# A transformer layer on eight cores: the bias moved from TensorE to VectorE, the residual load moved to GpSimd's queue, three staging buffers in place of four

## The chip, the cores and the metric

The kernel runs on all 8 cores of one Trainium2 chip, each core with one batch element and the whole set of weights. No core talks to another, but they share the chip's memory. The metric is the device time of the slowest core, in microseconds (us). The core profiled in detail is core 1.

## The reference

Per batch element, with x of 2048 rows (S) by 2048 columns (E) in f32:

```python
xn = _layernorm(x, axis=-1)
# attention: 16 heads of 128, rope on q and k, causal softmax
q = (x @ wq).reshape(B, S, H, D)      # here x is xn
...
attn = jax.nn.softmax(scores, axis=-1)
out = jnp.einsum('bhqk,bkhd->bqhd', attn, v).reshape(B, S, E)
return out @ wo
# ffn: ternary weights
scale = jnp.mean(jnp.abs(weight))
w_t = jnp.clip(jnp.round(weight / (scale + EPS)), -1.0, 1.0)
...
return jnp.einsum('bsi,oi->bso', x, w_ste) + bias
# the layer
x = x + attn_part + ffn_part
```

So the result is a sum of four things: the residual x, attention's output times wo, xn times the quantized ffn weight, and the bias, one value per column.

## The kernel before, in words

The kernel is written engine by engine: a Python planner appends closures to five lists (SyncE, ScalarE, VectorE, TensorE, GpSimd), and every instruction of an engine runs in the order in which it was appended. Semaphores carry all dependencies, each counted by the planner. The helper `dma` (line 150 issues a plain transfer, line 148 a transposing one) puts on the named engine's list the waits, then the transfer. A transfer that waits therefore holds up all that stands behind it on that engine.

**Start.** SyncE loads eight constants (rope tables c2 and s2 of 1 MB each, then six small ones) on one semaphore `c`, each after the one before has landed. GpSimd's queue holds the bias row `biasb`, then the first four tiles of x into `xst[0..3]` (128 rows, 1 MB each), then the weights of heads 0 and 1 (`wslq`, `wslk`, `wslv`, 0.5 MB each as bf16, cast on the way).

**Layernorm** (`plan_ln_tile`, 16 tiles). GpSimd loads x into `xst[b]`, b the tile's number mod 4, once the tile that used it last is done. ScalarE makes sum and sum of squares (L191, L198), VectorE mean and variance (L208 to L222), ScalarE the inverse root (L229, L236), VectorE the normalized bf16 tile `xnn` (L243), and SyncE transposes it by DMA into `xnT`, which stays in SBUF. VectorE's list begins with a wait for all constants, ahead of its first L208. Four tiles are planned ahead of head 0, and four more behind each of its chunks.

**Heads.** Each of 16 heads has four chunks of 512 rows: projections k, q, v from `xnT` and the head's weights (L474, L477) into the banks pA and pB, rope on VectorE, v transposed by DMA, then scores, Exp and the products with v. Between the chunks stand parts of the weight quantization: `plan_quantA_tile` (heads 2 to 5, ScalarE sums |w|) and `plan_quantB_tile` (heads 6 to 13, VectorE). Both load `wf` into the same `xst` buffers by GpSimd's queue. The quantized, transposed weight goes to DRAM as `wtT_scr`; the heads' outputs go to `outT_scr`, the last two heads' stay in `oTs`.

**Phase 2.** SyncE loads `oTh[0]` (rows 0 to 1023 of the heads' output), ScalarE's queue `oTh[1]`, 14 transfers each. The output is made in 16 chunks: two halves of the rows by eight column blocks of 256 (W2). Chunk idx needs `woc` (a block of wo, cast to bf16 on GpSimd's queue) and `wtc` (a block of the quantized weight, on SyncE's), two buffers each. `plan_ph2_weights(idx + 1)` stands in the lists ahead of the tiles of chunk idx, and its transfers wait until TensorE is done with chunk idx - 1, whose buffers they take. A chunk has eight tiles of 128 rows. For each tile SyncE loads `xsl`, the residual's 128x256 block (two buffers, each free when VectorE is done with its last tile), and TensorE makes 33 matmuls into one of two PSUM banks:

- L922, one matmul with one row: ones times the bias row, which starts the sum;
- L930, 16 matmuls of the heads' output and `woc`;
- L933 and L937, 16 matmuls of `xnT` and `wtc`.

VectorE adds `xsl` to the bank and writes `osl` (L953), ScalarE's queue stores `osl` to y. TensorE may write a bank again when VectorE has read it, so it runs two tiles ahead of VectorE and no more.

Of the kernel before, what the change touches and what calls it, by code (L numbers as in the profile page):

```python
# [8 lines left out]
F32 = mybir.dt.float32  # L9
# [5 lines left out]
E = 2048  # L15
# [24 lines left out]
def build_nc():  # L40
# [26 lines left out]
    with ctx:  # L67
# [8 lines left out]
        onrf = sb("onrfs", [1, 128], F32)  # L76
        biasb = sb("biasb", [1, E], BF16)
        st6 = sb("st6", [128, 24], F32)
        mv = [sb(f"mv{i}", [128, 2], F32) for i in range(4)]
        rstd = [sb(f"rstd{i}", [128, 1], F32) for i in range(4)]  # L80
        epsv = sb("epsv", [128, 1], F32)
        bias3 = sb("bias3", [128, 1], F32)
        accw = sb("accw", [128, 16], F32)
# [2 lines left out]
        thrv = sb("thrv", [128, 1], F32)  # L86
        nthrv = sb("nthrv", [128, 1], F32)
        oTs = [sb(f"oTs{i}", [128, S], BF16) for i in range(2)]
        ctx1 = ExitStack()
        sb1 = lambda n_, s_, d_: ctx1.enter_context(nc.sbuf_tensor(n_, s_, d_))  # L90
        xst = [sb1(f"xst{i}", [128, E], F32) for i in range(4)]
        xnn = [sb1(f"xnn{i}", [128, E], BF16) for i in range(2)]
        wtbf = [sb1("wtbf0", [128, E], BF16)] * 4
        wtTs = [sb1("wtTs0", [128, NT * 128], BF16)] * 4
# [66 lines left out]
        def _(e):  # L161
            e.memset(epsv[:, :], LN_EPS)
            e.memset(bias3[:, :], -3.0)
            e.wait_ge(sems["c"], consts_c)

        @on("tensor")
        def _(e):
            e.wait_ge(sems["c"], consts_c)

        xst_free = [("dv", 0), ("dv", 0), ("dv", 0), ("dv", 0)]  # L170
        xnn_free = [("txn", 0), ("txb", 0)]
        ln_state = {"prev_aggr": 0}
        ln_prev = [0, 0, 0, 0]

        def plan_ln_tile(tt):
            b = tt % 4
            b2 = tt % 2
            xs = "x%d" % b
            my_x = dma("gpsimd", xs,
                       (lambda tt=tt, b=b: (xst[b][:, :],  # L180
                        bass.AP(x_d.tensor, tt * 128 * E, [[E, 128], [1, E]]), False)),
                       extra_waits=[xst_free[b]])

            @on("scalar")
            def _(e, b=b, b2=b2, xs=xs, my_x=my_x, xf=xnn_free[b2], prev=ln_prev[b]):
                e.wait_ge(sems[xs], my_x)
                if xf:
                    e.wait_ge(sems[xf[0]], xf[1])
                if prev:
                    e.wait_ge(sems["dv"], prev)  # L190
                e.activation(out=xnn[b2][:, :], in_=xst[b][:, :], func=AF.Copy,  # L191
                             accum_out=mv[b][:, 0:1]).then_inc(sems["ac"], 1)
            ac_copy = bump("ac")

            @on("scalar")
            def _(e, b=b, b2=b2, ac_copy=ac_copy):
                e.wait_ge(sems["ac"], ac_copy)
                e.activation(out=xnn[b2][:, :], in_=xst[b][:, :], func=AF.Square,  # L198
                             accum_out=mv[b][:, 1:2]).then_inc(sems["ac"], 1)
            ac_sums = bump("ac")  # L200

            dv_m = bump("dv")
            dv_var1 = bump("dv")

            @on("vector")
            def _(e, b=b, ac_sums=ac_sums, dv_m=dv_m):
                e.wait_ge(sems["ac"], ac_sums)
                e.tensor_scalar(out=mv[b][:, 0:1], in0=mv[b][:, 0:1], scalar1=1.0 / E,  # L208
                                scalar2=None, op0=ALU.mult).then_inc(sems["dv"], 1)
                e.wait_ge(sems["dv"], dv_m)  # L210
                e.scalar_tensor_tensor(out=st6[:, b:b + 1], in0=mv[b][:, 0:1], scalar=-1.0,
                                       in1=mv[b][:, 0:1], op0=ALU.mult,
                                       op1=ALU.mult).then_inc(sems["dv"], 1)
            bump_chk = cnt["dv"]
            assert bump_chk == dv_var1

            dv_var2 = bump("dv")

            @on("vector")
            def _(e, b=b, dv_var1=dv_var1):  # L220
                e.wait_ge(sems["dv"], dv_var1)
                e.tensor_scalar(out=rstd[b][:, :], in0=mv[b][:, 1:2], scalar1=1.0 / E,  # L222
                                scalar2=st6[:, b:b + 1], op0=ALU.mult,
                                op1=ALU.add).then_inc(sems["dv"], 1)

            @on("scalar")
            def _(e, b=b, dv_var2=dv_var2):
                e.wait_ge(sems["dv"], dv_var2)
                e.activation(out=rstd[b][:, :], in_=rstd[b][:, :], func=AF.Ln,  # L229
                             bias=epsv[:, :]).then_inc(sems["ac"], 1)  # L230
            ac_ln = bump("ac")

            @on("scalar")
            def _(e, b=b, ac_ln=ac_ln):
                e.wait_ge(sems["ac"], ac_ln)
                e.activation(out=rstd[b][:, :], in_=rstd[b][:, :], func=AF.Exp,  # L236
                             scale=-0.5).then_inc(sems["ac"], 1)
            ac_rstd = bump("ac")

            @on("vector")  # L240
            def _(e, b=b, b2=b2, ac_rstd=ac_rstd):
                e.wait_ge(sems["ac"], ac_rstd)
                e.tensor_scalar(out=xnn[b2][:, :], in0=xst[b][:, :], scalar1=mv[b][:, 0:1],  # L243
                                scalar2=rstd[b][:, :], op0=ALU.subtract,
                                op1=ALU.mult).then_inc(sems["dv"], 1)
            dv_xn = bump("dv")
            xst_free[b] = ("dv", dv_xn)
            ln_prev[b] = dv_xn

            txs = "txn" if tt % 2 == 0 else "txb"  # L250
            xnn_free[b2] = (txs, dma("sync", txs,
                              (lambda tt=tt, b2=b2: (
                                  bass.AP(xnT, tt * 128, [[NT * S, 128], [S, NT], [1, 128]]),
                                  xnn[b2][:, :], True)),
                              extra_waits=[("dv", dv_xn)]))
# [8 lines left out]
        quantB_state = {"prev_sub": 0}  # L264

        def plan_quantA_tile(qt):
            b = qt % 4
            b2 = qt % 2
            xs = "x%d" % b
            my_x = dma("gpsimd", xs,  # L270
                       (lambda qt=qt, b=b: (xst[b][:, :],
                        bass.AP(wf_d.tensor, qt * 128 * E, [[E, 128], [1, E]]), False)),
                       extra_waits=[xst_free[b]])

            @on("scalar")
            def _(e, qt=qt, b=b, b2=b2, xs=xs, my_x=my_x):
                e.wait_ge(sems[xs], my_x)
                e.wait_ge(sems["txn"], xnT_ready)
                e.wait_ge(sems["txb"], xnT_ready)
                e.activation(out=xnn[b2][:, :], in_=xst[b][:, :], func=AF.Abs,  # L280
                             accum_out=accw[:, qt:qt + 1]).then_inc(sems["ac"], 1)
            qa_ac[qt] = bump("ac")
            xst_free[b] = ("ac", qa_ac[qt])
# [56 lines left out]
            return bump("dv")  # L340

        def plan_quantB_tile(qt, thr_dv):
            b = qt % 4
            xs = "x%d" % b
            my_x = dma("gpsimd", xs,
                       (lambda qt=qt, b=b: (xst[b][:, :],
# [537 lines left out]
        for idx in range(len(chunks)):  # L884
# [7 lines left out]
            if True:  # L892

                for ti in range(8):
# [3 lines left out]
                    syp = "sy%d" % tb  # L898
                    pp = ph2_psums[tb]
                    xsl_first = (half == 0 and ec == 0 and ti < 2)  # L900
                    xsl_ld = dma("sync", xsp,
                                 (lambda tt=tt, tb=tb, ec=ec: (xsl[tb][:, :],
                                  bass.AP(x_d.tensor, tt * 128 * E + ec * W2, [[E, 128], [1, W2]]),
                                  False)),
# [4 lines left out]
                    def _(e, pp=pp, ti=ti, tt=tt, ec=ec, ecb=ecb, wop=wop, wcp=wcp,  # L909
# [9 lines left out]
                        e.wait_ge(sems["bias"], bias_v)  # L919
                        if dv_gate:  # L920
                            e.wait_ge(sems["dv"], dv_gate)
                        e.matmul(pp[:, 0:W2], onr[:, :], biasb[0:1, ec * W2:(ec + 1) * W2],  # L922
                                 start=True, stop=False)
                        for it in range(NT):
                            if it >= H - 2:
                                lh = oTs[it % 2][:, tt * 128:(tt + 1) * 128]
                            else:
                                lh = bass.AP(oTh[half], it * 1024 + ti * 128,
                                             [[H * 1024, 128], [1, 128]])
                            e.matmul(pp[:, 0:W2], lh,  # L930
                                     woc[ecb][:, it * W2:(it + 1) * W2], start=False, stop=False)
                        for it in range(NT - 1):
                            e.matmul(pp[:, 0:W2],  # L933
                                     bass.AP(xnT, it * S + tt * 128, [[NT * S, 128], [1, 128]]),
# [8 lines left out]
                    wtc_used_pe[ecb] = pe_out  # L943


                    @on("vector")
                    def _(e, pp=pp, tb=tb, xsp=xsp, syp=syp, pe_out=pe_out,
                          xsl_ld=xsl_ld, osl_gate=osl_st[tb]):
                        e.wait_ge(sems["pe"], pe_out)
                        e.wait_ge(sems[xsp], xsl_ld)  # L950
                        if osl_gate:
                            e.wait_ge(sems[syp], osl_gate)
                        e.tensor_tensor(out=osl[tb][:, :], in0=pp[:, 0:W2], in1=xsl[tb][:, :],  # L953
                                        op=ALU.add).then_inc(sems["dv"], 1)
                    dv_out = bump("dv")
                    ph2_free_dv[tb] = dv_out
# [87 lines left out]
```

## Time and profile before

| | us |
|---|---|
| Three timed runs | 2002.83, 1991.86, 1933.22 (median 1991.86) |
| Profiled execution, its own time | 1938.87 |
| Its span on the slowest core (core 1) | 1937.1 |
| Spans of the eight cores | 1869.6 to 1937.1 |
| TensorE busy, core 1 | 1574.5 (81% of the span) |
| VectorE busy | 671.5 |
| ScalarE busy | 538.0 |

On core 1 the program falls into three parts: layernorm and its transposes with heads 0 and 1 (0 to about 300 us), the other heads (to 1353 us), and phase 2 (1353 to 1937 us). A busy share is an average over all three, so each part is read by itself. In rows, PE is TensorE, PEld its weight loads, DVE VectorE, ACT ScalarE, POOL GpSimd, and SPq, ACTq the DMA-issuing queues of SyncE and ScalarE. All DMAs issued by the helper carry its line, 150 or 148, and are told apart by their tiles.

### The profile page before, as it was taken

How to read it: one execution, taken by the hardware profiler on the slowest of the kernel's cores; microseconds unless marked ns; L12 is line 12 of the kernel's file. 1: busy time of each engine (PE TensorE's matmuls, PEld its weight loads, DVE VectorE, ACT ScalarE, POOL GpSimd, SP SyncE). 2: the span in 40 equal slices, each digit the busy share in tenths (PEclk: the TensorE clock that was granted, in tenths of full speed). 3: DMA queues.
4: the chain of work that ended last, by engine and by line, in shares of the span. 5: the costliest groups of instructions: out<-in, count | busy, mean ns of one | idle time of the engine just before them, and what ended most of it. 6: DMA issues, size and time to landing. Idle time of an engine off the chain costs nothing. (4 is left out here: it accounts for less than half of the span.)

```text
span 1937.1 us, 29502 instructions; the slowest of 8 cores (1869.6 to 1937.1 us)
## 1 busy us (share of the span) xinstructions
PE 1574.5 (81%) x9220; PEld 885.1 (46%) x9220; DVE 671.5 (35%) x1399; ACT 538.0 (28%) x897; POOL 100.4 (5%) x117
## 2 busy tenths in 40 slices
PE   0044359999999999999999999998369999999999
PEld 0011123444444444444444444443257787777777
DVE  0123243346445556546546645543000110101101
ACT  1311345463554353343344235144000000000000
POOL 2000001000101000000000000000000000000000
PEclk9986689999999999999999999999689999999999
DMA  9967729027536364465356245000954655555462
GB/s 191 117 83 73 134 47 161 28 82 131 91 92 98 87 123 72 98 115 79 93 115 107 63 71 85 20 9 8 232 109 104 140 124 130 126 132 126 109 153 66
DMA packets 350388, 194.93 MB, mean 101 GB/s; under 512 B 240163, under 2 KB 338468, under 8 KB 343844
## 3 DMA queue, kind: packets, MB, share of 16 engines
q0 software_dynamic: 139040, 92.29, 28.9%
q1 hardware_dynamic: 190756, 80.31, 20.2%
q10 hardware_dynamic: 20448, 20.46, 3.2%
q8 instruction: 85, 1.39, 0.3%
q14 instruction: 59, 0.48, 0.1%
HBM read 177.28 MB, written 32.51 MB: 108 GB/s over the span
## 5 line engine op out<-in xcount | busy, mean ns | idle before, releaser
L577 ACT ACTIVATE et<-pC,bias 128x512 bf16<-128x512 f32 (+3 forms) x240 | 149.9, 625 | 595.1 <-PE pC L564 594.0
L614 PE MATMUL pF<-et,onms 128*128 128x512 bf16 (+3 forms) x640 | 223.3, 351 | 16.1 <-ACT et L577 12.2
L474 PE MATMUL pA<-xnT,wslk 128*128 128x512 bf16 x480 | 115.6, 396 | 126.7 <-DMA xnT<-xnn 126.5
L474 PE MATMUL pB<-xnT,wslv 128*128 128x512 bf16 x480 | 115.0, 394 | 79.1 <-DVE prawk L489 79.1
L953 DVE TENSOR_TENSOR osl<-pA,xsl 128x256 f32<-128x256 f32 x64 | 27.2, 425 | 366.5 <-PE pA L937 183.1
L588 DVE TENSOR_TENSOR et<-et,trim 128x128 bf16<-128x128 bf16 x256 | 57.3, 225 | 269.7 <-ACT et L577 265.9
L616 PE MATMUL pG<-et,vh 128*128 128x512 bf16 (+3 forms) x384 | 135.8, 357 | 0.0
L577 ACT ACTIVATE et<-pD,bias 128x512 bf16<-128x512 f32 (+3 forms) x208 | 130.8, 629 | 2.0 <-PE pD L564 0.9
L474 PEld LDWEIGHTS pA<-xnT,wslk 128*128 128x128 bf16 x480 | 46.7, 101 | 183.8 <-issue 137.1
L564 PE MATMUL pC<-qTh,kTh 128*128 128x512 bf16 (+3 forms) x240 | 83.9, 349 | 55.9 <-ACT et L577 55.9
L577 ACT ACTIVATE et<-pH,bias 128x512 bf16<-128x512 f32 (+1 forms) x192 | 118.6, 618 | 2.0 <-PE pH L564 1.8
L930 PE MATMUL pA<-woc,oTh 128*128 128x256 bf16 x896 | 118.9, 289 | 0.0
L933 PE MATMUL pA<-wtc,xnT 128*128 128x256 bf16 x960 | 118.9, 278 | 0.0
L933 PE MATMUL pB<-wtc,xnT 128*128 128x256 bf16 x960 | 115.3, 273 | 0.0
L614 PEld LDWEIGHTS pF<-et,onms 128*128 128x128 bf16 x640 | 62.6, 98 | 114.2 <-issue 67.2
L474 PEld LDWEIGHTS pB<-xnT,wslv 128*128 128x128 bf16 x480 | 48.2, 101 | 141.2 <-issue 88.8
L930 PE MATMUL pB<-woc,oTh 128*128 128x256 bf16 x896 | 108.9, 273 | 0.0
L474 PE MATMUL pA<-xnT,wslq 128*128 128x512 bf16 x480 | 108.8, 379 | 0.0
L474 PE MATMUL pA<-xnT,wslv 128*128 128x512 bf16 x480 | 108.8, 379 | 0.0
L474 PE MATMUL pB<-xnT,wslq 128*128 128x512 bf16 x480 | 108.8, 379 | 0.0
L474 PE MATMUL pB<-xnT,wslk 128*128 128x512 bf16 x480 | 108.8, 379 | 0.0
L933 PEld LDWEIGHTS pA<-wtc,xnT 128*128 128x128 bf16 x960 | 96.1, 100 | 13.4
(97 smaller groups left out, 1956.6 us busy)
## 6 DMA issues: line engine op xcount, KB each, us to landing
xst<-wf POOLq DMA_DIRECT2D x32, 1024.0 KB, 12.1
xst<-x POOLq DMA_DIRECT2D x16, 1024.0 KB, 15.2
woc<-wo POOLq DMA_DIRECT2D x16, 1024.0 KB, 13.3
wtc<-wtT_scr SPq DMA_DIRECT2D x16, 1024.0 KB, 7.1
xsl<-x SPq DMA_DIRECT2D x128, 128.0 KB, 3.1
y<-osl ACTq DMA_DIRECT2D x128, 128.0 KB, 2.9
wslq<-wq POOLq DMA_DIRECT2D x16, 512.0 KB, 8.0
wslk<-wk POOLq DMA_DIRECT2D x16, 512.0 KB, 9.7
```

The costliest lines, as they stand in the source:

```text
L474: e.matmul(pp[:, 0:CW], wsl[:, it * 128:(it + 1) * 128], bass.AP(xnT, it * S + c * CW, [[NT * S, 128], [1, CW]]), start=(it == 0), stop=False)
L564: e.matmul(pc_[:, col0:CW], kTh[hb][:, kt * 128:(kt + 1) * 128], bass.AP(qTh[hb], cs0 + col0, [[S, 128], [1, n]]), start=True, stop=True). ...
L577: e.activation(out=et[slot][:, col0:CW], in_=pc_[:, col0:CW], func=AF.Exp, scale=INV_SQRT_D, bias=bias3[:, :]).then_inc(sems["ac"], 1)
L588: e.tensor_tensor(out=et[slot][:, col0:col0 + 128], in0=et[slot][:, col0:col0 + 128], in1=tri[:, :], op=ALU.mult).then_inc(sems["dv"], 1)
L614: e.matmul(pF[:, col0:CW], onm[:, :], et[slot][:, col0:CW], start=(kt == 0), stop=(kt == nkt - 1))
L616: e.matmul(pv[:, col0:CW], vh[hb][:, kt * 128:(kt + 1) * 128], et[slot][:, col0:CW], start=(kt == 0), stop=(kt == nkt - 1)).then_inc(sems[ ...
L930: e.matmul(pp[:, 0:W2], lh, woc[ecb][:, it * W2:(it + 1) * W2], start=False, stop=False)
L933: e.matmul(pp[:, 0:W2], bass.AP(xnT, it * S + tt * 128, [[NT * S, 128], [1, 128]]), wtc[ecb][:, it * W2:(it + 1) * W2], start=False, stop= ...
L953: e.tensor_tensor(out=osl[tb][:, :], in0=pp[:, 0:W2], in1=xsl[tb][:, :], op=ALU.add).then_inc(sems["dv"], 1)
```

## The change

Four edits, and what they bring with them.

1. `xst`, `mv` and `rstd` have three buffers in place of four, and all `% 4` of the tiles become `% 3`.
2. A tile `biasbc` (128 x 2048, bf16) holds the bias on all partitions. It is filled at the start: four matmuls of ones and a quarter of `biasb` into pH, each copied out by ScalarE, one after the other. They stand ahead of layernorm on both engines.
3. In phase 2 the bias matmul is gone, and VectorE adds `biasbc` in a second instruction behind the first. TensorE and the next `xsl` load wait for the second one.
4. The `xsl` loads are issued by GpSimd in place of SyncE.

```diff
-        xst = [sb1(f"xst{i}", [128, E], F32) for i in range(4)]
+        xst = [sb1(f"xst{i}", [128, E], F32) for i in range(3)]
...
+        biasbc = sb("biasbc", [128, E], BF16)
...
+        for j in range(4):
+            @on("tensor")
+            def _(e, j=j, bv=bias_v, pba=prev_bb_ac):
+                if j == 0:
+                    e.wait_ge(sems["c"], consts_c)
+                    e.wait_ge(sems["bias"], bv)
+                else:
+                    e.wait_ge(sems["ac"], pba)
+                e.matmul(pH[:, 0:512], onr[:, :], biasb[0:1, j * 512:(j + 1) * 512],
+                         start=True, stop=True).then_inc(sems["pe"], 1)
+            pe_bb = bump("pe")
+
+            @on("scalar")
+            def _(e, j=j, pe_bb=pe_bb):
+                e.wait_ge(sems["pe"], pe_bb)
+                e.activation(out=biasbc[:, j * 512:(j + 1) * 512], in_=pH[:, 0:512],
+                             func=AF.Copy).then_inc(sems["ac"], 1)
+            prev_bb_ac = bump("ac")
...
-            b = tt % 4
+            b = tt % 3
...
-                    xsl_ld = dma("sync", xsp,
+                    xsl_ld = dma("gpsimd", xsp,
...
-                        e.matmul(pp[:, 0:W2], onr[:, :], biasb[0:1, ec * W2:(ec + 1) * W2],
-                                 start=True, stop=False)
...
-                                     woc[ecb][:, it * W2:(it + 1) * W2], start=False, stop=False)
+                                     woc[ecb][:, it * W2:(it + 1) * W2], start=(it == 0), stop=False)
...
                         e.tensor_tensor(out=osl[tb][:, :], in0=pp[:, 0:W2], in1=xsl[tb][:, :],
+                                        op=ALU.add).then_inc(sems["dv"], 1)
+                        e.wait_ge(sems["dv"], dv_out1)
+                        e.tensor_tensor(out=osl[tb][:, :], in0=osl[tb][:, :],
+                                        in1=biasbc[:, ec * W2:(ec + 1) * W2],
                                         op=ALU.add).then_inc(sems["dv"], 1)
```

**GpSimd's queue in phase 2.** Before, from the first loads of phase 2 on (line 150 is the helper's; `waits` names the semaphores, `wo0` and `wo1` those of woc's own buffers, pe TensorE's):

```order
L150 DMA woc0<-wo 128x16x256 [waits so0,so1,sw0,sw1,tv0,tv1,tw0,tw1,txn,txb,pe,dv]
L150 DMA woc1<-wo 128x16x256 [waits so0,so1,sw0,sw1,tv0,tv1,tw0,tw1,txn,txb,pe,dv]
L150 DMA woc0<-wo 128x16x256 [waits pe,wo0]
```

In the changed kernel, around the load of chunk 2's block, which stands ahead of the eight tiles of chunk 1 (the helper's line is 151 now, xs0 and xs1 are the semaphores of the two `xsl` buffers, dv is VectorE's):

```order
L151 DMA xsl1<-x 128x256 [waits dv,xs1]
L151 DMA woc0<-wo 128x16x256 [waits pe,wo0]
L151 DMA xsl0<-x 128x256 [waits dv,xs0]
L151 DMA xsl1<-x 128x256 [waits dv,xs1]
L151 DMA xsl0<-x 128x256 [waits dv,xs0]
L151 DMA xsl1<-x 128x256 [waits dv,xs1]
L151 DMA xsl0<-x 128x256 [waits dv,xs0]
L151 DMA xsl1<-x 128x256 [waits dv,xs1]
L151 DMA xsl0<-x 128x256 [waits dv,xs0]
L151 DMA xsl1<-x 128x256 [waits dv,xs1]
L151 DMA woc1<-wo 128x16x256 [waits pe,wo1]
L151 DMA xsl0<-x 128x256 [waits dv,xs0]
```

The eight residual loads of each chunk have come to stand between two `woc` loads. On SyncE's queue they stood in the same way behind `wtc`; before, at the same place of the program:

```order
L150 DMA xsl1<-x 128x256 [waits dv,xs1]
L150 DMA wtc0<-wtT_scr 128x16x256 [waits sw0,sw1,pe,wc0]
L150 DMA xsl0<-x 128x256 [waits dv,xs0]
L150 DMA xsl1<-x 128x256 [waits dv,xs1]
L150 DMA xsl0<-x 128x256 [waits dv,xs0]
```

So a residual load leaves the queue behind one block load, and joins the queue behind the other.

**GpSimd's queue at the start.** Before, from the bias row on (x0 to x3 are the semaphores of the `xst` buffers, a load that waits for dv waits until VectorE has normalized the tile in that buffer):

```order
L150 DMA xst2<-x 128x2048
L150 DMA xst3<-x 128x2048
L150 DMA wslq0<-wq 128x16x128
L150 DMA wslk0<-wk 128x16x128
L150 DMA wslv0<-wv 128x16x128
L150 DMA wslq1<-wq 128x16x128 [waits wq]
```

And now:

```order
L151 DMA xst2<-x 128x2048
L151 DMA xst0<-x 128x2048 [waits dv,x0]
L151 DMA wslq0<-wq 128x16x128
L151 DMA wslk0<-wk 128x16x128
L151 DMA wslv0<-wv 128x16x128
L151 DMA wslq1<-wq 128x16x128 [waits wq]
```

The fourth tile's load has become one that waits for tile 0's layernorm, and all weights of heads 0 and 1 stand behind it.

## Rows read from the trace of the kernel before

**Rows 1.** Stretches: PE, PEld, DVE, ACT, POOL busy us (instructions), granted clock, DMA share, GB/s.

```profile
0.00:20.00 20.00, 0.00 (x0) 0.00 (x0) 0.09 (x2) 5.29 (x5) 6.44 (x12) 1.00 0.88 262
17.00:50.00 33.00, 0.00 (x0) 0.00 (x0) 0.00 (x0) 0.47 (x2) 3.43 (x3) 1.00 1.25 157
55.00:111.00 56.00, 0.00 (x0) 0.01 (x1) 6.39 (x13) 16.76 (x22) 2.15 (x4) 1.00 1.06 113
300.00:1353.00 1053.00, 978.39 (x4620) 437.72 (x4618) 538.50 (x1104) 455.18 (x782) 65.32 (x74) 0.99 0.45 84
1420.00:1937.00 517.00, 482.28 (x4078) 392.91 (x4076) 52.67 (x124) 0.00 (x0) 15.98 (x14) 0.98 0.54 120
```

**Rows 2.** Chain of waits, 1420 to 1937 us, its shares by line.

```profile
by line: DMA xsl<-x 23.0%; PE pA L930 18.1%; PE pB L930 16.8%; PE pA L933 15.4%; PE pB L933 14.9%; PE pA L922 2.1%; PE pB L922 1.9%; DMA y<-osl 1.4%; DVE osl L953 1.3%; issue 1.3%; PE pB L937 1.0%; SPq L150 1.0%; PE pA L937 1.0%; SPq L143 0
```

**Rows 3.** The same chain at one chunk boundary: start us, us, what.

```profile
1536.02 0.21 PE pB L922
1536.23 1.85 PE pB L930 x16
1538.08 1.64 PE pB L933 x15
1539.72 0.12 PE pB L937
...
1540.49 7.71 DMA xsl<-x
...
1548.36 0.43 DVE osl L953
...
1548.93 0.26 PE pA L922
```

**Rows 4.** Waits by total, 1420 to 1937 us: us, times, longest.

```profile
PE pA L922 <- DVE osl L953: 31.9, 15, 4.7
```

**Rows 5.** The page's DMA issues: transfers, KB each, median us from issue to landing.

```profile
woc<-wo POOLq DMA_DIRECT2D x16, 1024.0 KB, 13.3
wtc<-wtT_scr SPq DMA_DIRECT2D x16, 1024.0 KB, 7.1
xsl<-x SPq DMA_DIRECT2D x128, 128.0 KB, 3.1
```

**Rows 6.** DMA issues at two other boundaries, near 1471 and 1705 us: slowest and fastest.

```profile
woc<-wo POOLq DMA_DIRECT2D x1, 1024.0 KB, 15.9
...
woc<-wo POOLq DMA_DIRECT2D x1, 1024.0 KB, 12.1
```

**Rows 7.** GpSimd's DMA issues from 299.5 us, 1.16 us apart: first and third.

```profile
wslq<-wq POOLq DMA_DIRECT2D x1, 512.0 KB, 8.3
...
wslv<-wv POOLq DMA_DIRECT2D x1, 512.0 KB, 11.8
```

**Rows 8.** Chain of waits in phase 2: first tile behind the longest stop, then behind a shorter.

```profile
1416.96 3.52 PE pA L930 x16
1420.48 2.62 PE pA L933 x15
...
1446.68 3.33 PE pA L930 x16
```

**Rows 9.** TensorE behind the longest stop: stretch as in rows 1, and its first instruction.

```profile
1416.60:1420.40 3.80, 3.80 (x18) 2.52 (x19) 0.18 (x1) 0.00 (x0) 0.00 (x0) 0.50 0.50 145
...
1416.59 0.36 PE L922 MATMUL pA<-biasb,onrs 1*128 1x256 bf16 x1 [12.65 <-DVE osl L953]
```

**Rows 10.** The start in order of time: start us, us, engine, instruction.

```profile
20.13 0.33 SPq L150 DMA_DIRECT2D trim<-tri  x1
45.77 0.30 SPq L150 DMA_DIRECT2D onrs<-onr  x1
52.88 0.15 DVE L208 TENSOR_SCALAR mv<-mv 128x1 f32<-128x1 f32 x1 [51.65 <-DMA onms<-onm]
111.02 5.38 PE L474 MATMUL pA<-xnT,wslk 128*128 128x512 bf16 x15 [111.02 <-DMA xnT<-xnn]
```

More of the change, by code:

```diff
@@ L78, in build_nc @@
         st6 = sb("st6", [128, 24], F32)
-        mv = [sb(f"mv{i}", [128, 2], F32) for i in range(4)]
-        rstd = [sb(f"rstd{i}", [128, 1], F32) for i in range(4)]
+        mv = [sb(f"mv{i}", [128, 2], F32) for i in range(3)]
+        rstd = [sb(f"rstd{i}", [128, 1], F32) for i in range(3)]
         epsv = sb("epsv", [128, 1], F32)
@@ L164, in _ @@
             e.wait_ge(sems["c"], consts_c)
+        prev_bb_ac = 0
+        for j in range(4):
[15 more added lines that the diff above has]
+            prev_bb_ac = bump("ac")
+        biasbc_ac = cnt["ac"]
         @on("tensor")
@@ L168, in _ @@
             e.wait_ge(sems["c"], consts_c)
-        xst_free = [("dv", 0), ("dv", 0), ("dv", 0), ("dv", 0)]
+        xst_free = [("dv", 0), ("dv", 0), ("dv", 0)]
         xnn_free = [("txn", 0), ("txb", 0)]
         ln_state = {"prev_aggr": 0}
-        ln_prev = [0, 0, 0, 0]
+        ln_prev = [0, 0, 0]
         def plan_ln_tile(tt):
-            b = tt % 4
+            b = tt % 3
             b2 = tt % 2
@@ L266, in plan_quantA_tile @@
         def plan_quantA_tile(qt):
-            b = qt % 4
+            b = qt % 3
             b2 = qt % 2
@@ L342, in plan_quantB_tile @@
         def plan_quantB_tile(qt, thr_dv):
-            b = qt % 4
+            b = qt % 3
             xs = "x%d" % b
@@ L943, in build_nc, with _ @@
                     wtc_used_pe[ecb] = pe_out
+                    dv_out1 = bump("dv")
                     @on("vector")
-                    def _(e, pp=pp, tb=tb, xsp=xsp, syp=syp, pe_out=pe_out,
-                          xsl_ld=xsl_ld, osl_gate=osl_st[tb]):
+                    def _(e, pp=pp, tb=tb, ec=ec, xsp=xsp, syp=syp, pe_out=pe_out,
+                          xsl_ld=xsl_ld, osl_gate=osl_st[tb], dv_out1=dv_out1,
+                          bac=biasbc_ac):
                         e.wait_ge(sems["pe"], pe_out)
                         e.wait_ge(sems[xsp], xsl_ld)
+                        e.wait_ge(sems["ac"], bac)
                         if osl_gate:
```

## The prediction

> **What bounds the kernel now.** I looked first at the cores, whose spans go from 1869.6 to 1937.1 us; the slowest, core 1, sets the time, and the sum is made for it. Then the stretches: from 300 to 1353 us TensorE is busy for 978 of 1053 us at a granted clock of 0.99 [rows 1]. The heads are bound by TensorE, and no edit takes a matmul from them. From 1420 us on it is busy for 482 of 517 us [rows 1], but the chain of waits of that stretch is not all TensorE: 23.0% of it is the landing of `xsl` [rows 2], that is 118.9 us. Within a chunk these loads are hidden, so this is the price of the 14 chunk boundaries (into chunks 1 to 14; the last loads no further block), 8.49 us each.
>
> One boundary shows how it comes about [rows 3]. TensorE ends a chunk at 1539.84. `wtc` goes out on SyncE's queue and `xsl` right behind it, at 1540.49. TensorE has two banks to fill, so it makes two tiles of 0.21 + 1.85 + 1.64 + 0.12 = 3.82 us, 7.6 us together, and then stops until VectorE has read a bank. VectorE waits for `xsl`, which lands at 1548.20; the add starts at 1548.36, and TensorE goes on at 1548.93. With the mean landing of 8.49 us it goes on 0.65 + 8.49 + 0.16 + 0.43 + 0.14 = 9.87 us after the chunk's end, a stop of 2.2 us; 14 of these are 31 us, and the waits say 31.9 us [rows 4].
>
> **The bias matmuls (removed from TensorE).** Each costs 0.21 us on the chain [rows 3]. At a boundary the first two tiles end in a stop anyway, so six of eight count: 14 x 6 x 0.21 = 17.6 us. The first chunk (whose first four tiles end in a stop too, for ScalarE's queue [rows 9]) and the last add 12 x 0.21 = 2.5 us. Gain: 20.1 us.
>
> **The second add (VectorE).** There is no such row; the nearest is the first add, 0.43 us [rows 3], and I add 0.1 us for its wait. Within a chunk VectorE is idle (52.67 us busy of 517 [rows 1]), and the 0.5 us lies beside the other bank's tile. On the path it counts at each boundary, where the bank is given back by the second add, and once at the end: 0.5 us.
>
> **The residual load on GpSimd's queue.** It now stands behind `woc` in place of `wtc`. `wtc` lands 7.1 us after its issue, `woc` 13.3 us [rows 5]. Behind `wtc`, `xsl` took 7.71 us at the boundary shown [rows 3] and 8.49 on the mean, though its median over all tiles is 3.1 us [rows 5]: it landed 1.1 us (the boundary shown) to 1.9 us (mean) after `wtc`'s 7.1 were over. So it did not pass the transfer ahead of it. GpSimd's queue shows the same: of three weight slices issued 1.16 us apart the first lands 8.3 us after its issue and the third 11.8 us after its own, 5.8 us later than the first: they land one after the other [rows 7]. So I let `xsl` land 1.5 us behind `woc`. `woc` starts, like SyncE's loads, about 0.6 us after the chunk's end: 0.6 + 13.3 + 1.5 = 15.4. Then 0.16 + 0.43 + 0.10 + 0.43 + 0.14, and TensorE goes on 16.65 us after the chunk's end in place of 9.87: 6.8 us later, times 14 = 95 us. The stop grows from 2.2 to 16.65 - 2 x 3.6 = 9.4 us. Bounds: with `woc` at 12.1 us [rows 6] and `xsl` landing together with it TensorE goes on at 14.0 us, 58 us in all; with 15.9 us each time [rows 6] at 19.2 us, 131 us. Below both ends lies only rival A.
>
> All of this rests on the order in which one queue is served. The Trainium skill, page "DMA: Bandwidth & Descriptors", section "Queues, rings and completion order", says that a DMA engine takes turns between queues, but takes the descriptors of one queue's ring in order. By this rule the move of the load to another queue frees nothing: it changes which block is waited for, and picks the slower. The rows above agree on both queues.
>
> **The clock.** Behind a stop of 12.65 us TensorE was granted 0.50, its 1.2 GHz level [rows 9], and the tile took 3.52 + 2.62 us in place of 1.85 + 1.64, which it takes at 2.4 GHz: 2.65 us more [rows 3, 8]. Shorter stops, 4.7 us at most [rows 4], still cost it 1.3 to 1.7 us at six of the 14 boundaries (3.33 us for the first of them [rows 8]), 9 us together. With stops of 9.4 us I expect a slow start at all 14, between 1.3 and 2.65 us; I take 2.3, since 9.4 is nearer to 12.65: 32 - 9 = 23 us more (9 to 28).
>
> Phase 2: 95 - 20 + 23 + 0.5 = **98 us more** (58 - 20 + 9 = 47 to 131 - 20 + 28 = 139).
>
> **The start.** VectorE's first step of layernorm waited for the last constant until 51.65 us; six small ones took all the time from 20.13 us on [rows 10], while the weight slices kept the DMA engines at a share of 1.25 [rows 1]. The last three took 2 us each (45.77 to 51.65) [rows 10]. Now GpSimd's queue stops behind three tiles of x, so the small constants should be there at 20 + 6 x 2 = 32 us. Then the bias is spread: four rounds of a matmul and a copy, 1.35 us each by my estimate from a matmul, a copy of 0.6 us and two waits, 5.4 us. ScalarE's table load and tile 0's two passes follow, 5.3 us [rows 1]: VectorE starts near 43 us, 10 us earlier. But the six weight slices, which used the 33 us from 17 to 50, now stand behind tile 0 in the queue, and fall into the stretch in which transposes and loads already take a share of 1.06 [rows 1]. TensorE's first projection waited for these transposes until 111.02 [rows 10]. If the slices are hidden it starts at 101; if their 33 us come on top, at 134. I take 125, nearer to the latter because the stretch has no idle share: **14 us more** (-10 to +23). All that follows is shifted by it. In the last group of transposes tile 15 is no longer loaded ahead; I take 2 us.
>
> **Three buffers later.** Loads of `wf` wait for one tile more, and the weights of a head behind them. These are issued a whole head ahead of their use, and what they wait for now happens early in that head. TensorE's 978 of 1053 us [rows 1] cover it; nothing. If that cover were gone, a head would wait for some part of 12 us of landing.
>
> **Sum.** 1938.9 + 98 + 14 + 2 = 2053 us, against the profiled execution's own time. The three timed runs have their median 53 us above that execution. As half of what is measured lies there, the forecast is a little above the sum: 2060.
>
> **The rivals.**
> *A: `xsl` is served beside `woc`.* If GpSimd's queue serves a small transfer beside the large one ahead of it, `xsl` lands before TensorE has made its two tiles, as 3.1 us [rows 5] would allow, and the stops go. A chunk takes 8 x 3.60 = 28.8 us in place of 9.87 + 6 x 3.82 = 32.8: 56 us less for 14, and 2.5 us of bias and 9 us of slow starts less besides. With 16 us at the start: 1938.9 - 67 + 16 = 1888, faster. It decides if `xsl` lands within 7 us of a chunk's end. Rows 7 speak against it.
>
> *B: small transfers of GpSimd's queue are slow by themselves.* Within a chunk the next `xsl` of a bank is issued when both adds are done, and 7.2 - 1.0 - 0.7 = 5.5 us are left for it. The trace of before has no small transfer on this queue in a quiet stretch; on SyncE's it takes 3.1 us [rows 5]. If it took 7 us here, a pair of tiles would take 8.7 in place of 7.2 us: for some 45 pairs 65 us on top, 2118. The Trainium skill, same page, section "Anatomy of one DMA — SWDGE (gpsimd) path", gives about 2.0 us plus the bytes at 436 GB/s for a transfer on this path, by estimate 2.3 us for 128 KB, by which B would not happen; no run here shows it.
>
> *C: the stops stay as they are.* If `woc` landed as early as `wtc` does once `xsl` is gone from SyncE's queue, only the second add (14 x 0.53 = 7 us), the bias (-20) and the start (+16) are left: 1942. Against it: 256 KB of `xsl` beside the megabyte that lands for `woc` can't halve 13.3 us.
>
> **How the numbers follow.** The forecast has 0.74, A 0.07, B 0.12, C 0.07. The range takes the low ends of phase 2 and the start together (1938.9 + 47 - 10 = 1976); at the top it goes past B and the high ends (1938.9 + 139 + 23 = 2101), because the measured median may stand up to 53 us above: 1976 to 2140. About 2% is what a measurement of this kernel can tell from no change. Faster is A, within 2% is C, the rest is slower.
>
> **What would show it.** Right: phase 2's chain has `xsl` landings of 14 to 16 us after a chunk's end at 14 boundaries; TensorE's waits for VectorE there sum to some 130 us, and its clock falls at each; its first projection starts after 111 us, VectorE's first step of layernorm before 52 us. Wrong: landings under 8 us at the boundaries (A) or over 5.5 us within a chunk (B), or weight slices that delay no transpose.

## The result: 3.1% slower, and the profile after

| | before | after |
|---|---|---|
| Median of the timed runs, same chips | 2001.25 us (10 runs, 1933.22 to 2177.69) | 1998.47 us (10 runs, 1983.97 to 2172.85) |
| Profiled execution, its own time | 1938.87 | 1999.76 |
| Its span, slowest core | 1937.1 (core 1) | 1998.2 (core 7) |
| Spans of the eight cores | 1869.6 to 1937.1 | 1946.7 to 1998.2 |
| TensorE busy, slowest core | 1574.5 | 1556.9 |

The ratio is 1.0307, interval 1.0232 to 1.0381: slower. (The two medians look alike because several of the runs of before were disturbed by something that slows one die of the chip; the ratio leaves such runs out.) The forecast was 2060, from a sum of 2053; the profiled execution came to 1999.76, that is 61 us more than before where the sum said 114.

Three stretches of the changed kernel's core 7, in the columns of [rows 1]: the one up to the first projection, the heads, and phase 2.

```profile
55.00:91.00 36.00, 0.10 (x1) 0.14 (x2) 3.75 (x8) 9.00 (x12) 5.74 (x6) 1.00 1.55 142
...
291.00:1344.00 1053.00, 976.75 (x4610) 436.55 (x4608) 538.16 (x1104) 453.90 (x778) 63.10 (x72) 0.99 0.46 84
...
1420.00:1998.00 578.00, 457.10 (x3901) 394.90 (x3899) 103.26 (x246) 0.00 (x0) 81.25 (x135) 0.90 0.47 107
```

The second row answers to the heads' row of [rows 1]: 977 us busy of 1053 against 978, so nothing changed there. The last answers to its last row: TensorE is busy for 25 us less than before in a stretch that is 61 us longer, and its mean clock there went from 0.98 to 0.90. The loss is a loss of waiting, not of work.

The page's DMA issues of the changed kernel, against [rows 5]:

```profile
woc<-wo POOLq DMA_DIRECT2D x16, 1024.0 KB, 13.3
xsl<-x POOLq DMA_DIRECT2D x128, 128.0 KB, 3.0
wtc<-wtT_scr SPq DMA_DIRECT2D x16, 1024.0 KB, 8.0
```

The median of `xsl` is 3.0 us, as it was on the other queue. A reader who looked only here would find nothing wrong: 100 of 128 loads land in under 7 us, and the 28 behind a block load, two a boundary, don't move a median. The waits for 1420 to 1998 us show them, in the form of [rows 4]:

```profile
DVE osl L977 <- DMA xsl<-x: 181.9, 14, 16.0
...
PE pA L950 <- DVE osl L980: 117.3, 14, 11.3
```

TensorE waited 31.9 us for VectorE before [rows 4], now 117.3 us. VectorE in turn waited for `xsl` 14 times, once a boundary. The chain's shares, 1420 to 1998 us, against [rows 2]:

```profile
by line: DMA xsl<-x 29.5%; PE pA L950 18.4%; PE pA L953 14.5%; PE pB L950 14.2%; PE pB L953 13.3%; issue 3.2%; DVE osl L980 2.0%; DVE osl L977 2.0%; PE pB L957 0.9%; PE pA L957 0.9%; DVEq L973 0.1%; DVEq L974 0.1%; DVEq L976 0.1%; DVEq L979
```

One boundary in the same chain, to be laid beside [rows 3]:

```profile
1624.23 1.75 PE pB L950 x16
1625.98 1.64 PE pB L953 x15
1627.62 0.12 PE pB L957
...
1628.04 0.43 DVE osl L977
...
1628.57 0.43 DVE osl L980
...
1629.50 11.26 DMA xsl<-x
...
1640.99 0.43 DVE osl L977
...
1641.52 0.43 DVE osl L980
...
1642.09 3.57 PE pA L950 x16
1645.66 2.38 PE pA L953 x15
```

The timeline at the same place shows what stands between the two, and the windows view the clock that TensorE was granted afterwards:

```profile
1627.86 0.36 SPq L151 DMA_DIRECT2D wtc<-wtT_scr  x1
...
1628.34 1.17 POOL L151 DMA_DIRECT2D woc<-wo  x1 [5.19 <-PE pB L957]
...
1629.50 1.08 POOL L151 DMA_DIRECT2D xsl<-x  x2
```
```profile
woc<-wo POOLq DMA_DIRECT2D x1, 1024.0 KB, 12.0
```
```profile
1642.00:1645.40 3.40, 3.31 (x16) 2.42 (x17) 0.70 (x2) 0.00 (x0) 1.07 (x2) 0.50 0.46 130
```

The chunk ends at 1627.74. `woc` is issued at 1628.34 and lands 12.0 us later, at 1640.34. `xsl`, an eighth of its size, is issued behind it at 1629.50 and lands at 1640.76, 0.4 us behind `woc`. TensorE goes on at 1642.09, 14.35 us after the chunk's end, at a clock of 0.50 (1.2 GHz), and its 16 matmuls take 3.57 us in place of 1.75.

At the start (timeline of core 7, against [rows 10]) the picture is another one than predicted:

```profile
27.63 0.30 SPq L151 DMA_DIRECT2D onrs<-onr  x1
...
32.15 0.58 PE L176 MATMUL pH<-biasb,onrs 1*128 1x512 bf16 x1 [32.15 <-DMA onms<-onm]
...
43.05 0.15 DVE L230 TENSOR_SCALAR mv<-mv 128x1 f32<-128x1 f32 x1 [41.83 <-ACT xnn L220]
...
46.56 0.53 POOL L151 DMA_DIRECT2D xst<-x  x1 [42.76 <-DVE xnn L265]
47.08 1.19 POOL L151 DMA_DIRECT2D wslq<-wq  x1
...
78.16 1.63 POOL L151 DMA_DIRECT2D xst<-x  x3
```
```profile
90.89 4.91 PE L496 MATMUL pA<-xnT,wslk 128*128 128x512 bf16 x15 [52.63 <-DMA xnT<-xnn]
```

The first projection starts 20 us earlier than before, not 14 us later.

For the comparisons below, all eight cores of each profiled execution are taken together, since the slowest core is not always the same. "Phase 2" is a core's time from SyncE's first load of `oTh` to its end (the first matmul comes some 32 us later), as the mean of the eight cores; "first projection" is the mean of cores 1, 3, 5, 7, which set the time. Before: 577.3 us and 109.3 us. After: 641.4 us and 88.5 us. Each is from one execution; how far that can be trusted is seen in two kernels below whose phase 2 is that of before, 578.4 and 579.2 us.

### The profile page after: what moved, and what is told of

Read it like the earlier page. It is cut to its first block and busy times, and to the rows that moved or that the text cites. A ratio compares the mean times of both kernels' runs of the same rounds, so it can differ in the third digit from the quotient of the medians.

```text
span 1998.2 us, 29654 instructions; the slowest of 8 cores (1946.7 to 1998.2 us)
## 1 busy us (share of the span) xinstructions
PE 1556.9 (78%) x9096; PEld 892.7 (45%) x9096; DVE 724.4 (36%) x1527; ACT 541.2 (27%) x901; POOL 170.5 (9%) x245
## 3 DMA queue, kind: packets, MB, share of 16 engines
q0 software_dynamic: 145184, 109.07, 30.7%
q1 hardware_dynamic: 172324, 63.52, 16.6%
## 5 line engine op out<-in xcount | busy, mean ns | idle before, releaser
L950 PE MATMUL pA<-woc,oTh 128*128 128x256 bf16 x896 | 131.1, 308 | 170.6 <-DVE osl L980 134.6
L636 PE MATMUL pF<-et,onms 128*128 128x512 bf16 (+3 forms) x640 | 223.7, 351 | 16.6 <-ACT et L599 12.6
L950 PEld LDWEIGHTS pA<-woc,oTh 128*128 128x128 bf16 x896 | 96.6, 109 | 194.3 <-issue 174.5
L953 PE MATMUL pA<-wtc,xnT 128*128 128x256 bf16 x960 | 123.5, 284 | 0.0
L151 POOL DMA_DIRECT2D xsl<-x x128 | 68.8, 539 | 484.7 <-DVE osl L980 299.5
## 6 DMA issues: line engine op xcount, KB each, us to landing
woc<-wo POOLq DMA_DIRECT2D x16, 1024.0 KB, 13.3
```

Of the source, the lines that this page charges most:

```text
L151: e.dma_start(out=out, in_=in_).then_inc(sems[sem_name], 16)
L636: e.matmul(pF[:, col0:CW], onm[:, :], et[slot][:, col0:CW], start=(kt == 0), stop=(kt == nkt - 1))
L950: e.matmul(pp[:, 0:W2], lh, woc[ecb][:, it * W2:(it + 1) * W2], start=(it == 0), stop=False)
L953: e.matmul(pp[:, 0:W2], bass.AP(xnT, it * S + tt * 128, [[NT * S, 128], [1, 128]]), wtc[ecb][:, it * W2:(it + 1) * W2], start=False, stop= ...
```

## The experiments

**The theories.** *The queue's order:* `xsl` can't land before the block load that was issued ahead of it on its own queue, and GpSimd's block load is the slower one; that alone is the loss. *Rival, crowding:* the two block loads and `oTh` simply fill the DMA engines at a boundary, and a small load is late there on any queue. *Rival, the second add:* the pace of VectorE, with its two dependent adds and their wait, holds TensorE up. For the start: *the early constants* bring the gain, or *the later loads* do.

### The queue alone, both ways

In the changed kernel the load goes back to SyncE's queue, all else stays:

```diff
-                    xsl_ld = dma("gpsimd", xsp,
+                    xsl_ld = dma("sync", xsp,
```

> The changed kernel with the residual loads back on SyncE's queue: edits 1 to 3 without edit 4. Theory (the loss is the queue: xsl stands behind woc): the xsl landings at the 14 boundaries fall from 12.2 to some 8.5 us, TensorE goes on about 10.4 us after a chunk's end in place of 15.3, its clock falls at some 6 boundaries only, and phase 2 is 24 us shorter than in the kernel before (bias matmuls -31, second add +7); with the start 10 us earlier the time is 0.98 of the kernel before. Rival (the loss is the second add or the three buffers): phase 2 stays some 60 us longer than before, ratio near 1.03.

Measured: ratio to before 0.9924 (0.9875 to 0.9973), median 1918.20 us against 1934.39. Phase 2 takes 564.5 us, so this one word is worth 77 us of the changed kernel's 641.4. On core 5, the slowest, `xsl` lands 7.7 to 9.8 us after its issue at the boundaries, and 10 of the 14 starts are slow. Against before, phase 2 gains only 13 us where 24 were expected: TensorE is through with its two tiles sooner and waits longer, 45 us of stops a core on the mean where before had 28, with 7 slow starts where before had 4. The first projection stays at 88.3 us: the start has nothing to do with this queue.

The other way round, the kernel before with `xsl` on GpSimd's queue and the bias matmul kept:

```diff
-                    xsl_ld = dma("sync", xsp,
+                    xsl_ld = dma("gpsimd", xsp,
```

> The kernel before with the residual loads on GpSimd's queue: edit 4 alone. Theory: TensorE goes on 14.8 us after a chunk's end in place of 9.9, 69 us for 14 boundaries, and the clock falls at all 14, 22 us more: about 90 us slower than before, ratio 1.045; the start is as before. Rival (only the edits together cost): under 30 us.

Measured: ratio 1.0516 (1.0446 to 1.0586), median 2028.53 us. Phase 2 takes 658.6 us, 81 more than before; 90 were expected. On core 7 all 14 boundaries have a landing of 10.5 to 13.7 us and a slow start. The chain of that core at one of them:

```profile
1622.43 0.12 PE pB L937
...
1624.31 12.98 DMA xsl<-x
...
1637.45 0.43 DVE osl L953
...
1638.39 3.52 PE pA L930 x16
1641.91 2.52 PE pA L933 x15
```

There is one add here and no bias in VectorE, and the stop is as long. That ends the second add as the cause. The queue costs 77 us taken out of one kernel and 81 put into the other: it is the whole loss, and the other edits together are a small gain (ratio 0.9924).

### The residual ahead of the block load

If the order in the queue is the cause, a residual load put ahead of the block load should land early. In the changed kernel, `xsl` of a chunk's first two tiles is issued ahead of the next chunk's blocks:

```diff
+            for ti in range(2):
+                xsl_pre[half * 8 + ti] = plan_xsl(half, ec, ti)
             if idx + 1 < len(chunks):
                 plan_ph2_weights(idx + 1)
```

> The changed kernel, xsl still on GpSimd's queue, but the loads of a chunk's first two tiles stand ahead of the woc load. Theory (order within the queue is the cause): xsl lands 3 to 4 us after its issue at the boundaries, the stops go, a chunk takes 28 us, and phase 2 is some 80 us shorter than in the kernel before; ratio about 0.955. Rival (the cause is that three transfers share the DMA engines, or small transfers of this queue): xsl still lands over 8 us after its issue at the boundaries, stops of several us stay, ratio over 1.

Measured: ratio 0.9995 (0.9951 to 1.0039), median 1936.27 us; phase 2 559.8 us, but from 526 to 599 over the cores. The expectation (0.955) was missed by more than 4%. The timeline and the chain of core 7 say why:

```profile
1764.12 0.54 POOL L151 DMA_DIRECT2D xsl<-x  x1 [2.96 <-DVE osl L991]
1764.69 1.16 POOL L151 DMA_DIRECT2D woc<-wo  x1
1767.61 0.55 POOL L151 DMA_DIRECT2D xsl<-x  x1 [1.76 <-DVE osl L991]
```
```profile
1767.61 12.36 DMA xsl<-x
...
1780.20 0.43 DVE osl L988
```

The load that now goes out ahead of `woc` is no longer waited for; on core 7 the first of the two lands in 2.4 to 3.7 us. The next one, issued at 1767.61 when `woc` is 2.9 us under way, lands 12.4 us later: the wait has moved by two tiles, to a place where TensorE is again two tiles ahead and no more. At 14 places the landings are 9 to 12.6 us. How long the block takes sets the rest: from 1440 to 1860 us the waits of core 5, where `woc` lands in 10.8 us at the median, and of core 7, where it takes 13.8, are these:

```profile
PE pA L961 <- DVE osl L991: 18.1, 14, 2.4
```
```profile
PE pA L961 <- DVE osl L991: 54.1, 13, 5.4
```

Cores 2 to 5, with `woc` at 10.8 to 11.1 us, have 526 to 536 us of phase 2, the other four, with 13.8 to 15.1 us, 584 to 599; the slowest set the time. Why `woc` is quicker on the four wasn't looked into. So it isn't the boundary as such that makes a load slow. This run alone can't tell order from crowding: the late load is the first behind `woc`, but also the first issued while both blocks are under way. ScalarE's queue, below, tells the two apart.

The same on SyncE's queue, with `wtc` in the part of `woc`:

```diff
-            return dma("gpsimd", "xs%d" % tb,
+            return dma("sync", "xs%d" % tb,
```

> As the one before, but on SyncE's queue: the first two xsl loads ahead of wtc. Theory: same as there, stops gone, ratio about 0.955; the two queues differ by under 1%. Rival: GpSimd's queue is itself slower, so that this one is clearly faster than e3_ahead_gpsimd.

Measured: ratio 1.0047 (1.0009 to 1.0086), median 1941.83 us, phase 2 580.6 us. Core 1's timeline:

```profile
1512.03 0.33 SPq L151 DMA_DIRECT2D xsl<-x  x1
...
1512.61 0.38 SPq L151 DMA_DIRECT2D wtc<-wtT_scr  x1
...
1527.25 0.42 DVE L988 TENSOR_TENSOR osl<-pA,xsl 128x256 f32<-128x256 f32 x1 [8.28 <-DMA xsl<-x]
```

The same shift: the third tile's add has to wait, with landings of 10.7 to 12.5 us. And the page shows a new price:

```profile
wtc<-wtT_scr SPq DMA_DIRECT2D x16, 1024.0 KB, 13.9
```

`wtc` took 7.1 us before [rows 5]. Two things are new for it: two small loads stand ahead of it in the queue, and it goes out about 1.4 us behind `woc`, where it went out 0.5 us ahead of it. These runs don't tell the two apart. In either case this kernel is 16 us slower in phase 2 than the plain SyncE placement above (564.5).

### The start: three buffers, and the slices held back

Edit 1 alone, put into the kernel before:

```diff
-        xst = [sb1(f"xst{i}", [128, E], F32) for i in range(4)]
+        xst = [sb1(f"xst{i}", [128, E], F32) for i in range(3)]
...
-            b = tt % 4
+            b = tt % 3
```

> The kernel before with three buffers in place of four: edit 1 alone. Theory (the gain at the start comes from the weight slices that stand behind a waiting load, so that the small constants land undisturbed): the last constant at 31 us in place of 51, VectorE's first layernorm step near 32, first projection on the odd cores at 80 to 92 us in place of 106 to 111, phase 2 begins about 10 us earlier on the slowest core; phase 2 itself as before. Rival (the gain came with the bias work or by chance): first projection at 106 us or later on odd cores.

Measured: ratio 0.9946 (0.9923 to 0.9969), median 1918.38 us against 1928.97. VectorE's first step is at 30.7 us (51.6 before), the first projection at 78.6 us (109.3 before), phase 2 begins 19 us earlier on the odd cores (1330.6 against 1349.4) and takes 578.4 us, as before. So one buffer less is a gain of 0.5%, and the bias at the head of the program costs 10 us of the first projection (88.5 against 78.6).

Is it the early constants? Four buffers, and only the six weight slices wait for the constants:

```diff
-                              extra_waits=[("pe", gate_pe)])
+                              extra_waits=[("pe", gate_pe)] +
+                                          ([("c", consts_c)] if h == 0 else []))
```

> The kernel before, four buffers, but the first weight slices of head 0 wait for the constants. Theory: the same gain as with three buffers, since only the order at the start counts: last constant at 32 to 35 us, first projection at 75 to 92 us on odd cores. Rival (it is the slower drip of x tiles 4 to 7 through three buffers that relieves the transposes): constants early, but first projection on odd cores still at 100 us or later.

Measured: ratio 1.0010 (0.9962 to 1.0057), median 1942.11 us. VectorE starts early (33.2 us), but the first projection is at 100.3 us on the odd cores, and on the even ones at 99.6 us where before had 84.9. Half of the gain on one sort of core, a loss on the other. The transposes landed late. From core 3 of this kernel, then of the one with three buffers, the loads of x in the timeline, and below them the transposes among the DMA issues of 60 to 70 us:

```profile
57.33 2.22 POOL L150 DMA_DIRECT2D xst<-x  x3
...
xnT<-xnn SPq DMA_TRANSPOSE x1, 44.9
```
```profile
65.69 1.63 POOL L150 DMA_DIRECT2D xst<-x  x3
...
xnT<-xnn SPq DMA_TRANSPOSE x2, 14.9
```

In the one a transpose issued at 58.5 us took 44.9 us to land. In the other those issued at 57.3 and 67.0 took 16.7 and 13.2, 14.9 at the median. With four buffers three tiles of x go out from 57 us on, directly behind the slices of the second head; with three, they go out 8 us later. So the early constants are one part of the gain, and what comes with the third buffer itself is the other. That the other part is the later x loads is likely but not shown: the transpose issued at 67.0 stood right behind three of them, and took 13.2 us all the same. How a load delays a transpose (and why the odd cores more) wasn't taken apart.

### The residual on a queue without block loads

If a load is as late as the block ahead of it, it belongs on a queue that has no blocks. In phase 2 ScalarE's queue first loads `oTh[1]` and from then on only stores `osl`. In the changed kernel each `xsl` is issued there, right behind the store of the tile that frees its buffer; the first two stay with SyncE:

```diff
+            plan_xsl("sync")
+            plan_xsl("sync")
...
-                    xsl_ld = dma("gpsimd", xsp, ...
+                    xsl_ld = xsl_pre.pop(0)
...
                                      extra_waits=[("dv", dv_out)])
+                    plan_xsl("scalar")
```

> The changed kernel with the residual loads on ScalarE's queue (the first two on SyncE's), each right behind the store of the tile whose buffer it takes; no block load stands on that queue in phase 2. Theory (a residual load waits for the block load ahead of it on its queue, whichever tile it belongs to: with the first two ahead, the third waited): xsl lands in 3 to 6 us everywhere, the 14 stops go, a chunk takes 8 x 3.5 = 28 us, phase 2 comes to some 495 us in place of about 577 before and 640 changed, ratio about 0.95. Rival (the block loads crowd the DMA engines, so a residual load is late on any queue): landings over 7 us at the boundaries and stops of 2 us and more stay, ratio about 0.99.

Measured: ratio 0.9632 (0.9575 to 0.9689), median 1863.38 us against 1938.43; phase 2 518.5 us, 123 less than the changed kernel, where 495 us and a ratio of 0.95 were expected. Part of the 123 is order and not the queue's name: here too the first two loads of a chunk go out ahead of the blocks, as in the two kernels with `xsl` ahead (559.8 and 580.6), and it is against these that the queue without blocks gains 41 to 62 us. Over the cores TensorE's stops sum to 2 to 19 us, where those two had 18 to 65. Crowding is real all the same: in every chunk some load near the boundary takes 6.4 us or more, up to 11.8 on core 3, though no block is ahead of it on its queue. The waits of that core (1450 to 1800 us):

```profile
DVE osl L993 <- DMA xsl<-x: 125.1, 36, 8.0
...
PE pB L966 <- DVE osl L996: 16.6, 9, 3.3
```

VectorE waits 125 us for `xsl`, but TensorE only 16.6: most of these waits end before the second bank is full. `xsl` still has 23.8% of the chain there. At most 2 of the 14 starts of a core are slow.

With the bias matmul kept (three buffers, ScalarE's queue, no `biasbc`), the same diff put into the three-buffer kernel:

> As the one before, but with the bias matmul and without the second add: the kernel before with three buffers and the residual loads on ScalarE's queue. Theory: with the stops gone the bias matmul costs its full 0.32 us a tile, so a chunk takes 8 x 3.81 = 30.5 us and phase 2 is 35 to 40 us longer than in e7_scalar_queue; the start is 11 us earlier, since nothing is spread ahead of layernorm. Ratio about 0.965. Rival (the bias matmul is hidden or the second add costs as much): no difference in phase 2.

Measured: ratio 0.9733 (0.9661 to 0.9806), median 1881.53 us, phase 2 543.0 us (541 to 545 over the cores). Its chain from 1450 to 1800 us is TensorE alone:

```profile
by line: PE pB L946 24.4%; PE pA L946 24.2%; PE pB L949 21.5%; PE pA L949 21.5%; PE pA L938 2.8%; PE pB L938 2.8%; PE pA L953 1.4%; PE pB L953 1.4%
```

`xsl`, with 23.0% before [rows 2], is not in it. The stops and the slow starts behind them are worth 35 us (578.4 to 543.0, with the queue and the order that comes with it as the only difference). Here TensorE has hardly a stop left (0.6 us at most on a core), and the matmul of the bias has its full price, 0.32 us for each of 128 tiles, 41 us. Phase 2 is 25 us shorter without it in the kernel above, where 35 to 40 were expected, and 28 us in the next: both still stop for `xsl` now and then, since two tiles without the bias leave it less time to land. With `xsl` on SyncE's queue the same step was worth 14 us (578.4 to 564.5). The interval of this kernel's ratio reaches to 0.9806, so a gain of 2% is just not shown.

At last the bias spread is moved from the head of the program behind the first four tiles of layernorm, all else as two kernels above:

```diff
-        prev_bb_ac = 0
-        for j in range(4):
...
+            plan_ln_tile(tt)
+        prev_bb_ac = 0
+        for j in range(4):
```

> e7_scalar_queue with the spreading of the bias planned behind the first four layernorm tiles in place of ahead of them. Theory: VectorE's first layernorm step at 31 us in place of 41 to 43, first projection on odd cores at 77 to 82 us in place of 87 to 91, phase 2 as in e7_scalar_queue; 8 to 10 us less in all. Rival (transposes wait for DMA anyway): first projection no earlier than 87 us.

Measured: ratio 0.9611 (0.9562 to 0.9659), median 1858.76 us, the lowest of all. The first projection is at 76.4 us (87.9 with the bias ahead), VectorE's first step at 30.5. The two medians are 4.6 us apart where 8 to 10 were expected; by their intervals that difference is not shown.

| kernel | median us | ratio to before | first projection, odd cores | phase 2 |
|---|---|---|---|---|
| before | 1929 to 1938 on these chips | 1 | 109.3 | 577.3 |
| changed | 1998.47 | 1.0307 | 88.5 | 641.4 |
| changed, `xsl` on SyncE | 1918.20 | 0.9924 | 88.3 | 564.5 |
| before, `xsl` on GpSimd | 2028.53 | 1.0516 | 105.5 | 658.6 |
| changed, two `xsl` ahead of `woc` | 1936.27 | 0.9995 | 89.1 | 559.8 |
| the same on SyncE | 1941.83 | 1.0047 | 88.6 | 580.6 |
| before, three buffers | 1918.38 | 0.9946 | 78.6 | 578.4 |
| before, slices held back | 1942.11 | 1.0010 | 100.3 | 579.2 |
| changed, `xsl` on ScalarE | 1863.38 | 0.9632 | 87.9 | 518.5 |
| the same, bias matmul kept | 1881.53 | 0.9733 | 79.5 | 543.0 |
| the same, bias spread later | 1858.76 | 0.9611 | 76.4 | 514.7 |

## Why the prediction was right in its direction and too high

**What bounds phase 2: right.** The price of the boundaries was the right thing to look for, and the switch of one queue name moves phase 2 by 77 to 81 us with nothing else changed.

**The residual load: right in its mechanism, mis-sized.** The step had TensorE go on 16.65 us after a chunk's end. The 14 boundaries of core 7 have it at 15.35 us on the mean (13.4 to 18.3; the means of the other cores are 13.6 to 14.7): 5.5 us more than 9.87, not 6.8, and 77 us in place of 95. Two terms were too high. `woc` landed 13.0 us after its issue on the mean of the boundaries (12.7 at the median), not 13.3. And `xsl` landed 0.4 us behind it at the boundary shown, not 1.5. The 1.5 came from `wtc`'s median, taken against single `xsl` landings on the other queue: a difference of two unlike numbers. The 77 us lie between the step's bounds (58 and 131 us).

**The bias matmul: right in its direction, mis-sized.** A tile takes 3.50 us now, not 3.61: beside the 0.21 us of the row of its own [rows 3], the 16 matmuls behind it fell from 1.85 to 1.75 us. So it was worth 0.32 us, and by the prediction's own count of tiles (96 of them) 31 us, not 20; for the 92 from the first boundary on, 29. The price of an operation had been read from its own row alone.

**The clock: right, a little too high.** All 14 starts were slow, together 29 us; before, 9.6. That is 19.5 us, where the step had 23. **The second add: right**; it takes 0.43 us and 0.10 between. Together 77 - 29 + 19.5 + 0.5 = 68 us; from the first boundary on, core 7 took 69 us more than core 1 of before (571.6 against 502.4). The step said 98.

**The start: wrong, and this is the step that failed.** Its first half held: the last constant was there at 32 us, as said, the bias took 1.42 us a round (1.35), and VectorE began at 43.05 (43). The second half did not. It let most of the 33 us of the weight slices come on top, "because the stretch has no idle share", and put the first projection at 125 us; it began at 90.89. The share of 1.06 in [rows 1] was read as full. Here are 55 to 91 us of core 1 of before, and of core 3 with three buffers:

```profile
55.00:91.00 36.00, 0.00 (x0) 0.00 (x0) 6.39 (x13) 12.76 (x18) 2.15 (x4) 1.00 1.11 134
```
```profile
55.00:91.00 36.00, 10.59 (x38) 4.38 (x39) 7.10 (x14) 9.01 (x12) 5.87 (x6) 1.00 1.34 187
```

The share is a sum of the times of packets that can lie over each other, and 1.06 was no ceiling for it, nor 113 GB/s for the rate. On the odd cores the transposes together took no longer with the slices beside them: the first four of core 7 took 16.6, 17.1, 14.7 and 12.3 us. Before they took 12.5, 21.8, 18.0 and 19.7 there, beside loads of x, of which all but one now went out at 78.16 us. On the even cores the step was half right. The four took 10.5 to 14.2 us on core 0, against 8.1 to 9.3 before, and of the 9 us that VectorE began earlier 1.5 were left at the first projection.

The three-buffer run shows that the gain is real and belongs to edit 1 (109.3 to 78.6), the run with the slices held back that early constants are only a part of it; what makes a transpose quick or slow stays open. The start ended 10 us earlier at phase 2's beginning (1344.0 against 1353.9) where 16 us more were forecast: 26 us of the 53 by which the sum was too high. Phase 2's 98 against 69 is the other part (the stretch up to the first boundary gave 2 us back). The 7 us added to the sum for the timed runs weren't there either: the median of ten, 1998.47, lies next to the profiled execution. None of these errors cancelled another; all of them made the forecast too high. Of the 21 us gained at the first projection only 10 are left at phase 2, on the odd cores of the three-buffer run 19 of 31; where the rest goes in the heads I haven't traced.

**The rivals.** A (`xsl` served beside `woc`) fell: no landing at a boundary came within 7 us, and even a load issued 2.9 us behind `woc` took 12.4 us. B (small transfers of this queue are slow) fell: 3.0 us at the median. C fell: TensorE's waits went from 31.9 to 117.3 us. The rule of the Trainium skill, page "DMA: Bandwidth & Descriptors", section "Queues, rings and completion order", that one ring's descriptors are taken in order, agrees with what was read here at the boundaries, on both queues. By the estimate of 2.3 us for 128 KB, worked out from the same page's section "Anatomy of one DMA — SWDGE (gpsimd) path", B should not happen, and it did not; the median measured is 3.0 us.

## What to carry to other kernels

A small load that somebody waits for is as late as the last large load issued ahead of it on its queue, whichever engine's queue that is and whatever its own median says; moving it between two queues that both carry blocks only picks the block. Look for the queue that carries none: here that turned a loss of 3.1% into a gain of 3.7%, and the matmul taken from the bound engine then brought 25 to 28 us in phase 2 in place of 14. Putting the first small loads ahead of the block is not enough, since the next ones then stand behind it.

## What was not expected of the hardware

- Holding loads back made the start faster: with a queue stopped behind three tiles in place of four, the first projection came 31 us earlier (109.3 to 78.6 us on the odd cores, 84.9 to 75.2 on the even ones).
- A DMA transpose issued at 58.5 us, between the first and the second of three 1 MB loads, took 44.9 us to land; in another kernel one issued just behind three such loads took 13.2. What makes the difference isn't known.
- A matmul with one row costs 0.21 us, and the 16 behind it take 1.85 us in place of 1.75.
- The DMA engines' share was 1.06 where the transposes were late, and 1.55 where they weren't: it is no measure of what is left.
